# Odd columns of a pyramid level added on GpSimd, and one store in eight cut into uneven shares

## The reference

```python
def _gn(v, G=16, eps=1e-5):
    g = v.reshape(B_, G, C_ // G, H_, W_)
    m = jnp.mean(g, axis=(2, 3, 4), keepdims=True)
    s = jnp.var(g, axis=(2, 3, 4), keepdims=True)
    return ((g - m) / jnp.sqrt(s + eps)).reshape(v.shape)

for level in range(3):
    sh, sw = (H // 2 ** level, W // 2 ** level)
    temp = result[:, :, :sh, :sw]
    approx = conv(temp, K, padding='SAME')       # K = outer([.25,.5,.25], [.25,.5,.25])
    down = approx[:, :, ::2, ::2]
    result = result.at[:, :, :sh // 2, :sw // 2].set(down)

x = x + pyramid(_gn(x))
```

## Time and profile before

| what | value |
|---|---|
| median of 3 runs | 1299.66 us (1298.92 to 1299.93) |
| the profiled execution | 1298.75 us |
| its span, first to last instruction | 1297.0 us |
| PE, DVE, ACT, POOL busy | 93%, 86%, 88%, 37% of the span |
| moved by DMA | 537.01 MB, mean 414 GB/s |
| the chain that ended last, by engine | PE 55%, ACT 30%, issue 11% |
| mean granted clock of TensorE | 0.99 |

### The profile page before, as it was taken

How to read it: one execution, slowest core, us unless ns; L and a number is a source line. 1 busy time by engine, 2 the same in 40 slices (tenths; PEclk the granted TensorE clock), 3 DMA queues, 4 the chain that set the end, 5 groups by cost and what they waited for, 6 DMA issues and landing times.

```text
span 1297.0 us, 22951 instructions
## 1 busy us (share of the span) xinstructions
PE 1207.8 (93%) x7168; PEld 837.0 (65%) x7168; DVE 1114.1 (86%) x1664; ACT 1139.6 (88%) x1282; POOL 478.7 (37%) x1318
## 2 busy tenths in 40 slices
PE   5999999999999999999999999999999999999995
PEld 2666666666666666666666666666666666666664
DVE  5889889889889899899898888888888888898883
ACT  4998998998998998998998898889988889898995
POOL 4433433433433433433433343333333333333431
PEclk9999999999999999999999999999999999999998
DMA  9999999999999999999999999999999999999996
GB/s 385 395 416 424 423 422 424 423 423 423 424 423 423 423 423 423 423 424 422 424 422 422 423 424 421 422 421 408 418 421 417 407 419 416 407 416 423 411 397 257
DMA packets 106507, 537.01 MB, mean 414 GB/s; under 512 B 8192, under 2 KB 8192, under 8 KB 73728
## 3 DMA queue, kind: packets, MB, share of 16 engines
q1 hardware_dynamic: 53248, 268.45, 50.5%
q10 hardware_dynamic: 53248, 268.45, 49.9%
HBM read 268.44 MB, written 268.44 MB: 414 GB/s over the span
## 4 chain that ended last, share of the span: by engine, by line
PE 55%; ACT 30%; issue 11%; ACTq 2%; POOL 1%; DVE 0%; DVEq 0%; POOLq 0%
PE l_ps L373 17%; PE l_ps L376 17%; ACT xs L505 16%; PE l_ps L382 8%; ACT l L478 6%; PE l_ps L425 4%; ACT l L493 4%; PE var_ps L404 3%; ACT squares L466 2%; PE l_ps L427 2%; PE l_ps L426 2%; PE l_ps L428 2%; ACT l L477 2%; ACTq L515 1%; ACT junk L461 0%
## 5 line engine op out<-in xcount | busy, mean ns | idle before, releaser
L466 ACT ACTIVATE squares<-xs,negm 128x4096 bf16<-128x4096 f32 x128 | 474.8, 3710 | 4.1
L258 POOL TENSOR_TENSOR l<-l,col_fix 128x4 f32<-128x4 f32 x128 | 158.3, 1237 | 765.0 <-ACT l L478 765.0
L314 DVE SCALAR_TENSOR_TENSOR h<-xs 128x2048 f32<-128x2048 f32 x128 | 295.5, 2308 | 12.4 <-DMA xs<-x_dram 8.4
L322 DVE SCALAR_TENSOR_TENSOR h<-xs,h 128x2040 f32<-128x2040 f32 x128 | 291.5, 2277 | 0.0
L505 ACT ACTIVATE xs<-xs,negmr,r_plus 128x2048 f32<-128x2048 f32 x128 | 267.8, 2092 | 0.0
L301 DVE SCALAR_TENSOR_TENSOR xs<-l_ps,r,xs 64x256 f32<-64x256 f32 x256 | 123.0, 481 | 123.3 <-PE l_ps L428 121.5
L500 ACT ACTIVATE xs<-xs,negmr,r_plus 128x1024 f32<-128x1024 f32 x128 | 157.8, 1233 | 44.3 <-issue 44.3
L328 DVE SCALAR_TENSOR_TENSOR a<-h 128x1024 f32<-128x1024 f32 x128 | 157.8, 1233 | 4.4
L373 PE MATMUL l_ps<-a,w_odd 128*64 128x256 f32 x512 | 158.8, 392 | 0.0
L376 PE MATMUL l_ps<-a,w_odd 128*64 128x256 f32 x512 | 158.8, 392 | 0.0
L376 PE MATMUL l_ps<-a,w_even 128*64 128x256 f32 x512 | 152.3, 379 | 0.0
(11 more groups left out here) (88 smaller groups left out, 2404.5 us busy)
## 6 DMA issues: line engine op xcount, KB each, us to landing
xs<-x_dram SPq DMA_DIRECT2D x256, 1024.0 KB, 12.7
y_dram<-xs ACTq DMA_DIRECT2D x256, 1024.0 KB, 12.1
```

Source lines behind the costliest of these rows:

```text
L258: nc.gpsimd.tensor_tensor(col, col, col_fix[:, b], ALU.add).then_inc(l1_fixed, 1)
L314: nc.vector.scalar_tensor_tensor(h1[:, b], v[:, :, 0:W:2], 2.0, v[:, :, 1:W:2], ALU.mult, ALU.add).then_inc(h1_part, 1)
L322: nc.vector.scalar_tensor_tensor(h1[:, b, :, 1:W1], v[:, :, 1:W - 2:2], 1.0, h1[:, b, :, 1:W1], ALU.mult, ALU.add, accum_out=hsum[:, b:b + ...
L466: nc.scalar.activation(squares[:], xs[:, u % SLOTS, :], ACT.Square, bias=negm[:, b:b + 1], accum_out=sumsq[:, b:b + 1]).then_inc(sumsq_rea ...
```

## The change

GpSimd gets one new instruction per group. It adds, for all four rows of level 1 on a partition, each odd column to the odd column before it, 512 sums per partition, into a new buffer `pairs`. For column 0 there is nothing before, so level 1 (`l1_pad`) now has two columns of zeros ahead of each row. The instruction stands behind the edge terms of group u and ahead of the wait for group u's evacuation, and it works on group u - 1. Level 2 then takes four matmuls instead of six, two with even columns and, behind a new wait, two with the sums.

In slot 3 of the eight, the store of the top half is cut: the first channel as before over 128 partitions (512 KiB), the second over partitions 0 to 119 (480 KiB) and 120 to 127 (32 KiB). The other seven slots are stored as before.

```diff
+SPARED = 3
+PAD = 2
...
-        l1 = sb("l1", [P, 2, CG, RPP, W1])
+        l1_pad = sb("l1_pad", [P, 2, CG * RPP, PAD + W1])
+        l1 = l1_pad[:, :, :, PAD:].rearrange("p b (c s) w -> p b c s w", c=CG)
+        pairs = sb("pairs", [P, 2, CG * RPP, W2])
...
+        def stores_of(slot):
+            return 4 if slot == SPARED else HALVES
...
-                    sp.wait_ge(x_stored[slot], 16 * HALVES * lap)
+                    sp.wait_ge(x_stored[slot], 16 * stores_of(slot) * lap)
...
+            nc.gpsimd.memset(l1_pad[:].rearrange("p b r w -> p (b r) w")[:, :, 0:PAD], 0.0)
...
+            def add_pairs(base, k):
+                b = k % 2
+                if later(base, k, 2):
+                    pool.wait_ge(l2_ps_ready, base + k - 1)
+                odd = l1_pad[:, b]
+                nc.gpsimd.tensor_tensor(pairs[:, b], odd[:, :, PAD + 1:PAD + W1:2], odd[:, :, PAD - 1:PAD + W1 - 2:2],
+                                        ALU.add).then_inc(pairs_ready, 1)
...
                     nc.gpsimd.tensor_tensor(col_fix[:, b], negm[:, c].to_broadcast([P, TOP]), col_t[:],
                                             ALU.mult).then_inc(negm_e_ready, 1)
-
+                if exists(base, k):
+                    add_pairs(base, k)
+                if exists(base, u):
                     pool.wait_ge(negm_e_ready, n + 1)
                     pool.wait_ge(l1_ready, n + 1)
...
-                src = l1[:, b]
-                for s, (plain, twice) in enumerate(((w2_first, w2_first2), (w2_second, w2_second2))):
-                    nc.tensor.matmul(dst, twice[:], src[:, :, s, 0:W1:2], start=s == 0, stop=False)
-                    nc.tensor.matmul(dst, plain[:], src[:, :, s, 1:W1:2], start=False, stop=False)
-                    last = nc.tensor.matmul(dst[:, :, 1:W2], plain[:], src[:, :, s, 1:W1 - 2:2], start=False,
-                                            stop=s == 1)
+                even = l1[:, b, :, :, 0:W1:2]
+                pair = pairs[:, b].rearrange("p (c s) w -> p c s w", c=CG)
+                nc.tensor.matmul(dst, w2_first2[:], even[:, :, 0], start=True, stop=False)
+                nc.tensor.matmul(dst, w2_second2[:], even[:, :, 1], start=False, stop=False)
+                pe.wait_ge(pairs_ready, base + u + 1)
+                nc.tensor.matmul(dst, w2_first[:], pair[:, :, 0], start=False, stop=False)
+                last = nc.tensor.matmul(dst, w2_second[:], pair[:, :, 1], start=False, stop=True)
...
-                for f in range(HALVES):
-                    nc.scalar.dma_start(out_half[f][lap + back, slot], half_of(slot, f)).then_inc(x_stored[slot], 16)
+                dst, src = out_half[0][lap + back, slot], half_of(slot, 0)
+                if slot != SPARED:
+                    nc.scalar.dma_start(dst, src).then_inc(x_stored[slot], 16)
+                else:
+                    most = P - P // 16
+                    nc.scalar.dma_start(dst[:, 0], src[:, 0]).then_inc(x_stored[slot], 16)
+                    nc.scalar.dma_start(dst[0:most, 1], src[0:most, 1]).then_inc(x_stored[slot], 16)
+                    nc.scalar.dma_start(dst[most:P, 1], src[most:P, 1]).then_inc(x_stored[slot], 16)
+                nc.scalar.dma_start(out_half[1][lap + back, slot], half_of(slot, 1)).then_inc(x_stored[slot], 16)
```

More of the change, by code:

```diff
@@ L111, in pyramid_kernel @@
         l1_fixed = sem("l1_fixed")
+        pairs_ready = sem("pairs_ready")
         scaled = sem("scaled")
@@ L159, in _ @@
             for slot in range(SLOTS):
-                sp.wait_ge(x_stored[slot], 16 * HALVES * LAPS)
+                sp.wait_ge(x_stored[slot], 16 * stores_of(slot) * LAPS)
         @block.gpsimd
```

## The result

| | before | after |
|---|---|---|
| median of 6 runs on one chip, us | 1298.9 (1298.2 to 1299.9) | 1304.2 (1302.3 to 1307.4) |
| ratio, 95% interval | | 1.0042 (1.0028 to 1.0056) |
| profiled execution and its span, us | 1298.75, 1297.0 | 1303.47, 1301.7 |

What follows compares the result with a forecast made beforehand. Steps between the squares' starts, set by a PE-ScalarE loop, then slowed by store issues, were taken to bound it; 42.9 + 127 x 10.17 = 1334.5, plus 4 for the clock, 1338.5 span, gave 1341 us, range 1276 to 1375.

Steps and rivals of the forecast that it cites:

- Worth 0 for level 2's two matmuls: On PE, two matmuls fewer free up to 1.2 us a group, worth 0 because the bottom scaling covers level 2.
- The add's length: GpSimd's add of 512 columns was to take 1.09 us, with ends of 0.64 and 1.9 us.
- Held 1.0 us: GpSimd's add reading SBUF was to hold VectorE 1.0 us a group, 0.1 us less than its record.
- 0.55 us to spare in VectorE's loop: The loop through VectorE, the mean's matmul and level 3 could grow some 0.55 us before setting the group's time.
- The second loop: The loop through VectorE grows to 9.72 - 0.55 + 1.0 = 10.17 us a group and becomes the longest.
- the second stage: From 695.9 to 1202.1 us, 50 groups of 10.12 us lose 20.2 us against 9.72, ScalarE waiting for store issues.
- The rival with "some 0.7 us" of hold: VectorE held some 0.7 us gives 42.9 + 127 x 9.87 + 2.65 = 1299 us; part of no change, chance 0.07.
- The stores keep up at that pace (10.12): With groups 10.17 us apart, ScalarE's stores no longer fall behind and add nothing to the time.
- The clock, 4 us: PE pauses before level 3 in every group, so its clock falls at times: 4 us in all.
- the end of level 3's wait: Sign: level 3 on PE no longer waits for ScalarE's level-2 evacuation (L493).
- The squares' 10.1 to 10.3 us: Sign: the starts of the squares, one per group, lie 10.1 to 10.3 us apart from the beginning.
- an issue wait of "a few": Sign: ScalarE's wait for store issues before the beside scaling falls from 44.3 us to a few.

Runs made afterwards that it cites:

- both costs gone: The change without its store part, with the add moved forward to where VectorE waits and works from PSUM, against the kernel before: 1299.3 us, 0.9998.
- the cut at 125: Kernel before with the store part alone, one slot of eight, quarter cut at 125 partitions and a rest of 3: 1351.5 us, 1.0388.
- the cut of six slots: Kernel before with the quarter cut into 120 and 8 partitions in six of eight slots: 1335.5 us, 1.0261.
- the control: Kernel before with the top store of six of eight slots cut by image into two stores of all 128 partitions, equal shares: 1301.6 us, 1.0020.

## Why the prediction was wrong

- *Worth 0 for level 2's two matmuls:* right; with both costs gone the time is that of before (0.9998). *The add's length*, 1.09 us forecast: right at 1.05. Its 1.75 ns a column agrees with (1936 - 1046) / 512 = 1.74, from the adds of 1024 and of 512 columns without the store part, though the longer one reads neighbouring columns and the shorter every second one.
- *Held 1.0 us:* too much. The record less 0.1 was taken; it is the record less 0.2, 0.84 us.
- *0.55 us to spare in VectorE's loop:* too little. The idle time of 0.38 before level 3 begins at the modelled end of the mean's matmul. From start to start, L357 to L425 was 0.75 us and L379 to L448 is 0.25 now, so 0.50 was to spare there; and L379 starts 0.06 us behind the sum where L357 started 0.22. That is 0.66, and 9.72 - 0.66 + 0.84 = 9.90; the trace has 9.85.
- *The second loop "is then the longest", 42.9 + 127 x 10.17:* **the step that failed.** Two errors of 0.1 to 0.2 us made 10.17 of 9.85 us, and that is the difference between lying above and below the late engine's pace. Behind it stands an error of form: the second stage was treated as a loss of 20.2 us on top of the loop. It is a second bound, and the kernel takes the larger of the two: 1299 us for the late engine, 1275 us for the loop before, 1291 with the add. A group may grow by (1299 - 1275) / 127 = 0.19 us before the end moves, and the add makes it 0.12. The rival with "some 0.7 us" of hold came to 1299 us, near the 1300.2 us that the add by itself measures, but by the same sum and so by luck.
- *"The stores keep up at that pace (10.12), so nothing comes on top from them":* the second wrong term, 0 against the measured 4.0 us (2.5 to 5.6). That the kernel became slower, as forecast, is this term's doing and not the add's, so the direction was right by luck. The prediction weighed only the engine that is spared. It did not ask which engines take the rest: the first eight, and the late one is among them (four late landings in the cut slot). Its reading that a few engines lag and not all was right; it is one.
- *The clock, 4 us:* not seen. PE pauses some 1.4 us in every group, and the granted clock is 1.00 up to 963 us.
- Of the signs: the add's length, the mean waiting for VectorE (127 times) and the end of level 3's wait (17 left of 127) came as told. VectorE's four additions grew by 0.78 us on average, not by 1.0. The squares' 10.1 to 10.3 us, landings within 25 us (up to 34.4 after 1000 us) and an issue wait of "a few" (20.4) did not come.

## What to carry to other kernels

A stage in which transfers push back gives a pace; multiply it by all the groups before pricing anything else. If that comes near the whole span, the transfers are a bound of their own, and work added below it costs nothing until the loop passes it, as work taken away brings nothing. And when a transfer is cut so as to spare one engine, first find which engine is late, and look at where the remainder goes. The landings of the single shares in a trace show it before anything is changed.

## What the hardware showed unasked

- Of sixteen DMA engines that get equal shares, one is late from the first laps on; in the cut at 125 it is one of the two that get a share of the 125 and none of the rest of 3. A 4 KiB row more on it costs 0.19 us of the end (0.12 for each of the 22 on the first engine); sparing the last engine brought nothing. Why one is late, no run shows. The Trainium skill, DMA: Bandwidth & Descriptors, section "Latency and other measured facts", names engines 7 and 15 (counted from 0, so the eighth and the sixteenth) as usually slower and, as a best guess, puts it down to DMAs that GpSimd issues. The queues here belong to the sync engine and ScalarE, and neither the sixteenth engine nor the eighth is the late one by the times and landings of the cuts.
- A store more of the same bytes costs 0.026 us of the end (96 of them 2.5 us). Four or five in nearly every group push ScalarE back from the first groups on: the cut of six slots had 129.4 us of issue wait, the control 52.2 us, by the waits of each (us, times, longest):

```profile
ACT xs L504 <- issue: 129.4, 101, 4.1
```

```profile
ACT xs L504 <- issue: 52.2, 61, 3.2
```
